# The first chunk's projection is woven with the state tiles of the other three chunks

## The chip, the cores and the metric

One core of one Trainium2 chip runs the whole program. The metric is the device time of one execution in microseconds (us). Engines are named as in the profile: PE (TensorE), ACT (ScalarE), DVE (VectorE), POOL (GpSimd), SP (SyncE, which here only issues DMAs). About 0.5% of this kernel's time is what a measurement of it can tell from no change.

## The reference, cut to what matters

```python
x = x + attn(cond(x, itok_B_0_15, W), attention weights in 4 bits with scales)   # x is 32 x 64 x 1024
x = x + ffn(cond2(x, ...), ...)
# cond: out[b,d,t] = sum over c of x[b,c,t] * W[condition[b]][c,d]: "states", one 64 x 64 block per batch row
# attn: q, k, v = states @ dequantized weights; rope; causal softmax over 64 positions; output projection
```

The change lies wholly in the beginning: the states, and the first projection of attention. Everything from the first attention step on, and the whole of the second line, is as it was.

## The kernel before, in words

The 2048 tokens are four chunks of 512. The states of a chunk are eight tiles of 128 x 512, numbered n = 8c + k over all chunks (n = 0 to 31). A state tile goes through three engines: PE makes it in a PSUM bank with four fp32 matmuls (L1420; a record counts two passes for each); ACT writes its fp16 part (L1166, count `cond_hi`), DVE the fp16 remainder (L636, count `cond_split`), and then the bank is free. Seven banks take turns.

Each chunk needs a scale before ACT may convert its first tile: DVE takes the largest magnitude of the chunk's x (`chunk_max`, L544 on y), POOL reduces it over partitions (L499), DVE makes a power of two of it in five tiny steps (`chunk_scale`, L615 and L548 to L551). The 4-bit weights of the first value head are dequantized by DVE, ACT, DVE in turn (L535, L1143, L540). The weights of the first query and key units come as ten integer pieces that ACT converts (`first_int`, L1151).

The first projection multiplies the first chunk's states by five units of weights ("k" and four query heads; units 0 to 4), eight products each. A product is two fp16 matmuls (L1435, L1437) into the unit's bank; after each of the first seven, ACT rescales the bank in place (L1182), and the next product waits for it. Two units run side by side in 24 rounds: unit 0 in rounds 0 to 7, 1 in 4 to 11, 2 in 8 to 15, 3 in 12 to 19, 4 in 16 to 23. Units 0 and 3 share a bank, so do 1 and 4. In rounds 20 to 23 PE adds a block of the values, 24 matmuls (L1447). DVE rotates each finished unit (rope: L704, L714, L716, L761, L752, L765; six instructions); for unit 3 ACT takes one of the six. Between them DVE takes the largest magnitudes of a weight matrix of the second half, eight loads through two buffers (`absmax` of `wb_stage`, L544 on work); SP issues load k when the reduction k - 2 is done (L419). After all eight, L1008 closes this stage on DVE, and DVE goes on to the first attention step.

All of these are streams written out by hand, one per engine, in order; semaphores tie them. POOL, after the four reductions of L499, fills y with zeros, a chunk at a time (L507), each once that chunk's states are made. SP issues the loads in order too: x by chunks (L344), the blocks of W for each chunk (L324, a DMA for every half block, after a register load), the pieces of the value head (L355, L356) and the integer pieces (L386).

What matters most of the order before is in PE's stream: all 32 state tiles, then a wait for the last remainder, then the rounds:

```python
pe.wait_ge(S["cond_split"], NC * KT)
for r in range(ROUNDS):
```

Of the kernel before, what the change touches and what calls it, by code (L numbers as in the profile page):

```python
# [12 lines left out]
P = 128  # L13
KT = H // P
# [39 lines left out]
def build(nc, x, cond_rep, ids_rep, seq_rep, len_rep, cond_w, s_q, s_q_cols, s_o_cols, s_k, s_v, s_o, q_q, q_k, q_v, q_o,  # L54
# [8 lines left out]
    with ctx:  # L63
# [175 lines left out]
        def col(n, k=1):  # L239
            return sc[:, n:n + k]  # L240
# [57 lines left out]
            return ((lambda part: w2h[:, part, :], w2_t, col(SC2 + 2)),  # L298
                    (lambda part: wrh[:, part, :, :].rearrange("p k e -> p (k e)"), small[:, 256:320], col(SC2 + 1)))

        cond_banks = [pj[0], pj[1], ex, cx[0], cx[1], sa, sbk]

        cond_banks = [pj[0], pj[1], ex, cx[0], cx[1], sa, sbk]

        def cond_bank(n):
            return cond_banks[n % len(cond_banks)]

        def ctx_src(e):
            return cx[e][:, :].rearrange("p (m s) -> p m s", s=SEQ)
# [19 lines left out]
        def _(sp):  # L329
# [18 lines left out]
            def load_piece(g, i):  # L348

                rows = 4 * P * i  # L350
                shape = "p (k n) -> p k n"
                src = q_v[rows:rows + 4 * P, ds(g * HD, HD)].rearrange("(k p) n -> p k n", p=P)
                scale = s_v[4 * i:4 * i + 4, ds(g * HD, HD)].partition_broadcast(P)
                need(sp, S["dq_scaled"], g * PIECES + (i - 1))
                sp.dma_start(stage[:, i, 0, :].bitcast(i32).rearrange(shape, k=4), src).then_inc(staged[i], 16)  # L355
                sp.dma_start(stage[:, i, 1, :].rearrange(shape, k=4), scale).then_inc(staged[i], 16)  # L356
# [25 lines left out]
            def load_first_ints(b):  # L382

                for p in range(*INT_BATCHES[b]):
                    dst = int_first[:, p, :] if p < 8 else int_stage[p % 2]
                    sp.dma_start(dst.rearrange("p (k n) -> p k n", k=4), int_source(0, p)).then_inc(int_first_in[b], 16)  # L386

            def load_scales(g):
                src = s_q_cols[ds(g * HD, HD), :]
                if not isinstance(g, int):  # L390
                    sp.wait_ge(S["sc_step"], g * 4)
                sp.dma_start(sc_raw[:, :], src).then_inc(S["sc_raw_in"], 16)
# [4 lines left out]
            for c in range(NC):  # L397
                with sp.Fori(CT * c, CT * (c + 1)) as i:
                    load_cond(sp, i, 0, c)
                    if c >= ACT_CHUNKS:  # L400
                        load_cond(sp, i, 1, c)
                if c + 1 < NC:
                    load_x(c + 1)
                if c == 0:
                    load_scales(0)
                    load_piece(0, 0)
                    load_piece(0, 1)
                if c < len(INT_BATCHES):
                    load_first_ints(c)
            for dst, src in ((cos_t, rope_cos), (sin_t, rope_sin), (mask_t, neg_mask), (id16, ident16)):  # L410
                sp.dma_start(dst[:, :], src).then_inc(S["consts_in"], 16)
            load_out_scales(0)
# [109 lines left out]
        def _(dve):  # L522
# [8 lines left out]
            def dequant_scale(g, i):  # L531
                slot = i % 2
                dve.wait_ge(staged[slot], 32 * g + 32)
                need(dve, S["w_ready"], PIECES * g + (i - 1))
                dve.scalar_tensor_tensor(out=w32[:, slot, :], in0=stage[:, slot, 0, :].bitcast(i32), scalar=-8.0,  # L535
                                         in1=stage[:, slot, 1, :], op0=ALU.add, op1=ALU.mult).then_inc(S["dq_scaled"], 1)
# [24 lines left out]
            def scales_inverted(g):  # L561

                dve.wait_ge(S["sc_raw_in"], 16 * g + 16)
                dve.tensor_single_scalar(sc_inv[:, :].bitcast(i32), sc_raw[:, :].bitcast(i32), 0x7FFFFFFF,
                                         ALU.bitwise_and).then_inc(S["sc_step"], 1)
                dve.wait_ge(S["sc_step"], 4 * g + 1)
                for n, lo, hi in ((1, 0, KT), (0, KT, NU * KT)):
                    dve.tensor_scalar(sc_safe[:, lo:hi], sc_inv[:, lo:hi], col(FLOOR + n), col(FLOOR2 + n), ALU.is_lt,
                                      ALU.mult).then_inc(S["sc_step"], 1)
                dve.wait_ge(S["sc_step"], 4 * g + 3)  # L570
                dve.tensor_tensor(sc_safe[:, :], sc_safe[:, :], sc_raw[:, :], ALU.add).then_inc(S["sc_step"], 1)
                dve.wait_ge(S["sc_step"], 4 * g + 4)
                dve.reciprocal(sc_inv[:, :], sc_safe[:, :]).then_inc(S["sc_inv"], 1)
# [33 lines left out]
            def chunk_max(c):  # L607
                dve.wait_ge(x_in[c], 16)
                absmax(stat[:, T_X + c:T_X + c + 1], y[:, CT * c:CT * (c + 1), :].rearrange("p i n -> p (i n)")).then_inc(S["stat_x"], 1)
# [15 lines left out]
            dve.wait_ge(S["w_scales_ready"], 1)  # L625
            chunk_max(0)
            chunk_scale(0)
            for c in range(NC):

                for k in range(KT):  # L630
                    n = c * KT + k
                    if k == (KT // 4 if c == 0 else 0) and c + 1 < NC:
                        chunk_max(c + 1)
                    dve.wait_ge(S["cond_hi"], n + 1)
                    t = slice(CH * c, CH * (c + 1))
                    dve.scalar_tensor_tensor(out=hid[:, 1, k, t], in0=cond_bank(n)[:, :], scalar=col(SH + c),  # L636
                                             in1=hid[:, 0, k, t], op0=ALU.mult, op1=ALU.subtract).then_inc(S["cond_split"], 1)
                if c == 0:
                    scales_inverted(0)
                    unit_ratios(0, 0, 3)  # L640
                    unit_ratios(0, 3, NU)
                if c + 1 < NC:
                    chunk_scale(c + 1)
                if c == 0:
                    dequant_scale(0, 0)
                    dequant_scale(0, 1)
                    dequant_split(0, 0)
                    dequant_split(0, 1)
            def score_factors():

                link(dve.tensor_scalar(col(A, NC), col(ISH, NC), 1.0 / QKV_DOWN, None, ALU.mult))
# [341 lines left out]
                    ahead = (g, c + 1) if c + 1 < NC else (None if last else (g + 1, 0))  # L993
                    step((g, c), ahead, None if first and c == 0 else (g, c - 1), between, pieces)

            score_factors()
            for u in range(NU - 1):
                rope_cos((0, 0), u)
                rope_sin((0, 0), u)
                rope_add((0, 0), u)  # L1000
                if u in (0, 1, 2):
                    rope_high((0, 0), u)
                rope_split((0, 0), u)
                for k in (2 * u, 2 * u + 1):
                    dve.wait_ge(wb_in[k % 2], 16 * (k // 2 + 1))
                    absmax(wbmax[:, k:k + 1], wb_stage[k % 2]).then_inc(S["wb_read"], 1)
            dve.wait_ge(S["wb_read"], WB_STATS)
            dve.reduce_max(stat[:, T_WB:T_WB + 1], wbmax, X).then_inc(S["stat_wb"], 1)  # L1008
            dve.wait_ge(S["y_zero"], NC)
# [128 lines left out]
        def _(act):  # L1138
# [19 lines left out]
                with act.Fori(CT * c, CT * (c + 1)) as i:  # L1158
                    load_cond(act, i, 1, c)

            for c in range(NC):
                act.wait_ge(S["h_scale_ready"], c + 1)
                for k in range(KT):
                    n = c * KT + k
                    act.wait_ge(S["cond_done"], n + 1)
                    act.activation(hid[:, 0, k, CH * c:CH * (c + 1)], cond_bank(n)[:, :], ACT.Copy,  # L1166
                                   scale=col(SH + c)).then_inc(S["cond_hi"], 1)
                act.wait_ge(S["w_scales_ready"], 1)
                if c == 0:
                    for i in range(PIECES):  # L1170
                        dequant_hi(0, i)
                else:
                    for p in range(*INT_BATCHES[c - 1]):
                        first_int(p)

            def rescale(p4, u, j):

# [165 lines left out]
            for r in range(ROUNDS):  # L1343
                for u, j in quanta(r):
                    if j < KT - 1:
                        rescale((0, 0), u, j)
                if r in (22,):
                    rope_high((0, 0), {22: 3}[r])
            group(0, first=True)
            with act.Fori(1, NKV - 1) as g:  # L1350
                group(g)
# [57 lines left out]
        def _(pe):  # L1409
            mm = nc.tensor.matmul  # L1410

            for c in range(NC):
                pe.wait_ge(x_in[c], 16)
                pe.wait_ge(wc_in[c], 16 * CB)
                for k in range(KT):
                    n = c * KT + k
                    if n >= len(cond_banks):
                        pe.wait_ge(S["cond_split"], n - len(cond_banks) + 1)
                    for i in range(CT):
                        last = mm(cond_bank(n)[:, P * i:P * (i + 1)], y[:, CT * c + i, P * k:P * (k + 1)],  # L1420
                                  wc[:, CT * c + i, :], start=True, stop=True)
                    last.then_inc(S["cond_done"], 1)

            PARTS = ((0, 0), (0, 1), (1, 0))

# [251 lines left out]
                    step((g, c), (g, c + 1) if c + 1 < NC else (None if last else (g + 1, 0)),  # L1677
                         None if first and c == 0 else (g, c - 1), turn if last and c == NC - 1 else nothing)

            pe.wait_ge(S["consts_in"], 64)  # L1680
            pe.wait_ge(S["cond_split"], NC * KT)
            for r in range(ROUNDS):
                for u, j in quanta(r):
                    quantum((0, 0), u, j)
                if r >= ROUNDS - CT:
                    value_block((0, 0), r - (ROUNDS - CT))
            group(0, first=True)
            with pe.Fori(1, NKV - 1) as g:
                group(g)
# [160 lines left out]
```

## Time and profile before

| what | value |
|---|---|
| median of 3 runs (lowest, highest) | 1920.22 us (1913.91, 1923.56) |
| profiled execution: its time, its span | 1917.04 us, 1915.0 us |
| PE, DVE, ACT, POOL busy over the span | 90%, 83%, 73%, 3% |
| mean granted clock of PE | 0.976 |
| states: first matmul to last remainder | 13.45 to 80.0 us |
| first projection: first product to the end of its stage on DVE | 80.10 to 117.98 us |

Times in the trace are counted from the start of the span. A share of busy time is an average over the whole span; the change concerns the first 118 us of it, where the shares are others (the table of stretches below). A PE matmul's record holds its pipeline, so that two that follow each other overlap; the pitch, from one start to the next, is what PE spends.

### The profile page before, as it was taken

To read this page: it belongs to the slowest core of one execution; us is meant where nothing else is said; L and a number is where in the kernel's file an instruction comes from. 1 tells how busy PE (TensorE), PEld (TensorE's weight loads), DVE (VectorE), ACT (ScalarE), POOL (GpSimd) and SP (SyncE) were. 2 spreads that over 40 slices of the span, in tenths; PEclk is the share of its full clock that TensorE was granted. 3 is DMA by queue.
4 is the path that set the end of the run, shared out by engine and by line. 5 is a ranking of instruction groups with operands and counts; after the bars stand their busy time and mean duration, and the time that the engine had idled before them with its cause. 6 is when DMAs were issued, how large, how long until landed. Compare 5 with 4: busy or idle time off the path is not lost. (4 is left out here: it accounts for less than half of the span.)

```text
span 1915.0 us, 38654 instructions
## 1 busy us (share of the span) xinstructions
PE 1722.9 (90%) x14306; PEld 942.5 (49%) x14306; DVE 1585.7 (83%) x2670; ACT 1394.6 (73%) x2361; POOL 55.6 (3%) x50
## 2 busy tenths in 40 slices
PE   3689999998999999999989999999999777779999
PEld 3435555544454455445545544454555455554444
DVE  6598999998999899989998998989998868992222
ACT  2568888988888888888888988888988527960000
POOL 0200000000000000000000000000000001320000
PEclk8799999999999999999999999999999978999999
DMA  7321111020103010200111020103020230111111
GB/s 212 100 78 35 34 46 46 1 69 12 46 1 78 4 45 19 61 25 24 34 47 46 2 75 6 46 1 78 12 58 11 89 110 23 40 40 45 44 44 44
DMA packets 118063, 87.67 MB, mean 46 GB/s; under 512 B 13404, under 2 KB 108004, under 8 KB 117860
## 3 DMA queue, kind: packets, MB, share of 16 engines
q1 hardware_dynamic: 117220, 84.83, 15.0%
q8 instruction: 128, 2.10, 0.5%
q14 instruction: 75, 0.61, 0.1%
q10 hardware_dynamic: 640, 0.13, 0.0%
HBM read 76.55 MB, written 8.39 MB: 44 GB/s over the span
## 5 line engine op out<-in xcount | busy, mean ns | idle before, releaser
L1182 ACT ACTIVATE pj<-pj,ratio 128x512 f32<-128x512 f32 x865 | 576.4, 685 | 108.1 <-PE pj L1437 102.3
L1435 PE MATMUL pj<-hid,wts 128*128 128x512 f16 x1024 | 392.1, 383 | 67.1 <-DVE pj L804 25.0
L1437 PE MATMUL pj<-hid,wts 128*128 128x512 f16 x1024 | 390.3, 381 | 0.0
L1191 ACT ACTIVATE sbk<-sbk,wts 128x512 f32<-128x512 f32 x384 | 262.4, 683 | 41.5 <-PE sbk L1504 36.6
L1191 ACT ACTIVATE sa<-sa,wts 128x512 f32<-128x512 f32 x384 | 261.1, 680 | 24.1 <-PE sa L1504 23.9
L1435 PEld LDWEIGHTS pj<-hid,wts 128*128 128x128 f16 x1024 | 99.8, 97 | 237.2 <-ACT pj L1182 72.7
L1447 PEld LDWEIGHTS tp<-wts,hid 128*128 128x128 f16 x3072 | 181.7, 98 | 32.5 <-issue 3.5
L1447 PE MATMUL tp<-wts,hid 128*128 128x128 f16 x3072 | 192.5, 219 | 0.5
L1437 PEld LDWEIGHTS pj<-hid,wts 128*128 128x128 f16 x1024 | 100.6, 98 | 76.6 <-issue 1.1
L704 DVE SCALAR_TENSOR_TENSOR work<-pj,ratio,cos_t 128x512 f32<-128x512 f32 x128 | 95.5, 746 | 45.0 <-PE pj L1437 35.8
L1182 ACT ACTIVATE ex<-ex,ratio 128x512 f32<-128x512 f32 x193 | 128.1, 664 | 3.8 <-PE ex L1437 1.2
L795 DVE SCALAR_TENSOR_TENSOR y<-sa,wts,y 128x512 f32<-128x512 f32 x128 | 95.1, 743 | 27.2 <-PE sa L1504 27.2
L761 DVE TENSOR_TENSOR work<-work 128x512 f32<-128x512 f32 x160 | 109.6, 685 | 1.7
L1502 PE MATMUL sa<-cb,wts 128*128 128x512 f16 x256 | 97.6, 381 | 8.8 <-DVE y L795 6.5
L795 DVE SCALAR_TENSOR_TENSOR y<-sbk,wts,y 128x512 f32<-128x512 f32 x128 | 95.6, 747 | 11.9 <-PE sbk L1504 10.9
L1502 PE MATMUL sbk<-wts 128*128 128x512 f16 x256 | 98.8, 386 | 7.3 <-DVE y L795 7.3
L1502 PE MATMUL sa<-wts 128*128 128x512 f16 x256 | 98.4, 384 | 7.6 <-DVE y L795 7.5
L1502 PE MATMUL sbk<-cb,wts 128*128 128x512 f16 x256 | 97.8, 382 | 4.4 <-ACT sbk L1191 4.4
L714 DVE SCALAR_TENSOR_TENSOR work<-pj,ratio,sin_t 64x512 f32<-64x512 f32 x128 | 96.7, 755 | 4.1
L1435 PE MATMUL ex<-hid,wts 128*128 128x512 f16 x256 | 98.0, 383 | 1.0 <-ACT ex L1182 1.0
L1504 PE MATMUL sa<-wts 128*128 128x512 f16 x256 | 98.3, 384 | 0.0
L1504 PE MATMUL sbk<-wts 128*128 128x512 f16 x256 | 98.2, 383 | 0.0
(243 smaller groups left out, 3184.5 us busy)
## 6 DMA issues: line engine op xcount, KB each, us to landing
wts<-qo_d SPq DMA_DIRECT2D x64, 256.0 KB, 3.2
y<-x_d SPq DMA_DIRECT2D x7, 2048.0 KB, 7.9
wts<-qq_d SPq DMA_DIRECT2D x35, 256.0 KB, 3.1
int_even<-qq_d SPq DMA_DIRECT2D x29, 256.0 KB, 2.9
out_d<-y SPq DMA_DIRECT2D x12, 512.0 KB, 2.6
work<-qv_d SPq DMA_DIRECT2D x16, 256.0 KB, 7.5
work<-sv_d SPq DMA_DIRECT2D x16, 256.0 KB, 9.5
work<-wb_d SPq DMA_DIRECT2D x8, 512.0 KB, 4.4
```

The costliest lines, as they stand in the source:

```text
L704: dve.scalar_tensor_tensor(out=rope_sum_of(u), in0=src, scalar=ratio[:, last:last + 1], in1=tables(cos_t, CB), op0=ALU.mult, op1=ALU.mult)
L714: dve.scalar_tensor_tensor(out=b[0:half], in0=src[half:HD], scalar=ratio[half:HD, last:last + 1], in1=sin_t[half:HD, :].unsqueeze(1).broad ...
L761: dve.tensor_tensor(ra[:, u % 2, :], ra[:, u % 2, :], rb[:, :], ALU.add).then_inc(S["rope_sum"], 1)
L795: dve.scalar_tensor_tensor(out=dst, in0=out_bank[t % 2][:, :], scalar=o_last[:, at:at + 1], in1=dst, op0=ALU.mult, op1=ALU.add).then_inc(y ...
L1182: act.activation(unit_bank[u][:, :], unit_bank[u][:, :], ACT.Copy, scale=ratio[:, KT * u + j:KT * u + j + 1]).then_inc(u_scaled[u], 1)
L1191: act.activation(out_bank[t % 2][:, :], out_bank[t % 2][:, :], ACT.Copy, scale=o_ratio[:, REP * t + h:REP * t + h + 1]).then_inc(o_scaled[ ...
L1435: mm(bank[:, :], w_int[:, u, j, :], hid[:, 0, j, CH * c:CH * (c + 1)], start=j == 0, stop=False, skip_group_check=True)
L1437: mm(bank[:, :], w_int[:, u, j, :], hid[:, 1, j, CH * c:CH * (c + 1)], start=False, stop=True, skip_group_check=True).then_inc(u_done[u], 1)
L1447: last = mm(shared[:, P * i:P * (i + 1)], hid[:, lw, k, CH * c + P * i:CH * c + P * (i + 1)], w_v[:, lh, k, :], start=(k == 0 and (lw, lh) ...
L1502: mm(out_bank[lane][:, :], w_out[:, h, P * t:P * (t + 1)], cbs[c % 2][:, 0, h, :], start=h == 0, stop=False, skip_group_check=True)
L1504: mm(out_bank[lane][:, :], w_out[:, h, P * t:P * (t + 1)], cbs[c % 2][:, 1, h, :], start=False, stop=True, skip_group_check=True).then_inc ...
```

## The change

Only the first chunk's eight tiles come ahead of the first projection. The other 24 (n = 8 to 31) stand in its 24 rounds, one a round, behind the round's products, on PE, ACT and DVE alike. They take four banks in turn (cx1, sa, sbk, cx0) which the projection doesn't use. With them go the integer pieces, the dequantization of the value weights (round 10), the scales of chunk 2 (round 5) and chunk 3 (round 13), the rotation of units 0, 1, 2 (rounds 8, 12, 16) and four of the eight reductions of the weight matrix (rounds 20 to 23). On SP the four loads of the value pieces move from behind x of chunk 1 to behind the integer pieces of the second batch.

```diff
-        cond_banks = [pj[0], pj[1], ex, cx[0], cx[1], sa, sbk]
+        cond_first = [pj[0], pj[1], ex, cx[0], cx[1], sa, sbk, cx[0]]
+        cond_later = [cx[1], sa, sbk, cx[0]]
 
         def cond_bank(n):
-            return cond_banks[n % len(cond_banks)]
+            return cond_first[n] if n < KT else cond_later[n % 4]
...
                 if c == 0:
                     load_scales(0)
+                if c < len(INT_BATCHES):
+                    load_first_ints(c)
+                if c == 1:
                     load_piece(0, 0)
                     load_piece(0, 1)
-                if c < len(INT_BATCHES):
-                    load_first_ints(c)
...
+            for n in range(KT):
+                cond_lo(n)
+            scales_inverted(0)
+            unit_ratios(0, 0, 3)
+            unit_ratios(0, 3, NU)
+            chunk_max(1)
+            chunk_scale(1)
...
+            for r in range(ROUNDS):
+                cond_lo(KT + r)
+                if r == 5:
+                    chunk_max(2)
+                    chunk_scale(2)
+                if r == 10:
+                    dequant_scale(0, 0)
+                    dequant_scale(0, 1)
+                    dequant_split(0, 0)
+                    dequant_split(0, 1)
+                if r == 13:
+                    chunk_max(3)
+                    chunk_scale(3)
+                if r in (8, 12, 16):
+                    first_rope(r // 4 - 2)
+                if r >= 20:
+                    wb_max(r - 20)
+            score_factors()
+            first_rope(3)
+            for k in range(4, WB_STATS):
+                wb_max(k)
...
+            for n in range(KT):
+                cond_high(n)
+            for p in range(2):
+                first_int(p)
...
+                cond_high(KT + r)
+                if r % 4 >= 2 and r < 16:
+                    first_int(2 + 2 * (r // 4) + r % 4 - 2)
+                if r == 10:
+                    act.wait_ge(S["w_scales_ready"], 1)
+                    dequant_hi(0, 0)
+                    dequant_hi(0, 1)
...
+                if n >= KT - 1:
+                    pe.wait_ge(S["cond_split"], n - 3)
...
+            for n in range(KT):
+                cond(n)
+            pe.wait_ge(S["cond_split"], KT)
             for r in range(ROUNDS):
                 for u, j in quanta(r):
                     quantum((0, 0), u, j)
+                cond(KT + r)
                 if r >= ROUNDS - CT:
                     value_block((0, 0), r - (ROUNDS - CT))
+            pe.wait_ge(S["consts_in"], 64)
+            pe.wait_ge(S["cond_split"], NC * KT)
             group(0, first=True)
```

PE's stream before, where the first chunk's eighth tile is made (hid is the states, cb the blocks of W, y is x, wts the weights):

```order
L1420 MATMUL pj0<-cb,y 128x128 x4
L1420 MATMUL pj1<-cb,y 128x128 x4
L1420 MATMUL ex<-cb,y 128x128 x4
L1420 MATMUL cx0<-cb,y 128x128 x4
L1420 MATMUL cx1<-cb,y 128x128 x4
```

The same place now, in lines of the changed kernel (L1442 makes a state tile, L1457 and L1459 are a product):

```order
L1442 MATMUL cx0<-cb,y 128x128 x4
L1457 MATMUL pj0<-hid,wts 128x512
L1459 MATMUL pj0<-hid,wts 128x512
L1442 MATMUL cx1<-cb,y 128x128 x4
L1457 MATMUL pj0<-hid,wts 128x512
L1459 MATMUL pj0<-hid,wts 128x512
L1442 MATMUL sa<-cb,y 128x128 x4
```

Before, 24 more tiles came there ahead of the first product; now a product stands ahead of each of them.

DVE's stream before at the end of the stage: the last rotation, its two reductions, L1008, and the first instruction of the attention step:

```order
L704 SCALAR_TENSOR_TENSOR work<-pj0,ratio,cos_t 128x512
L714 SCALAR_TENSOR_TENSOR work<-pj0,ratio,sin_t 64x512
L716 SCALAR_TENSOR_TENSOR work<-pj0,ratio,sin_t 64x512
L761 TENSOR_TENSOR work<-work 128x512
L765 TENSOR_TENSOR qb<-work,qb 128x8x64
L544 TENSOR_REDUCE stat<-work 128x1 x2
L1008 TENSOR_REDUCE stat<-stat 128x1
L704 SCALAR_TENSOR_TENSOR work<-pj1,ratio,cos_t 128x512
```

DVE's stream now, from the last two remainders on (L633 a remainder, L646 the first of the five score factors, L699 to L760 the rotation, L1025 what L1008 was):

```order
L633 SCALAR_TENSOR_TENSOR hid<-sbk,sc,hid 128x512
L544 TENSOR_REDUCE stat<-work 128x1
L633 SCALAR_TENSOR_TENSOR hid<-cx0,sc,hid 128x512
L544 TENSOR_REDUCE stat<-work 128x1
L646 TENSOR_SCALAR sc<-sc 128x4
...
L699 SCALAR_TENSOR_TENSOR work<-pj0,ratio,cos_t 128x512
...
L760 TENSOR_TENSOR qb<-work,qb 128x8x64
L544 TENSOR_REDUCE stat<-work 128x1 x4
L1025 TENSOR_REDUCE stat<-stat 128x1
```

Two reductions stood behind each rotation; now the first four stand between the last remainders and the other four behind the last rotation.

## Rows read from the trace of the kernel before

**Rows 1.** Busy time by stretch: PE, PEld, DVE, ACT, POOL, then PEclk, DMA share, GB/s.
```profile
60.00:80.00 20.00, 10.99 (x72) 10.53 (x72) 14.54 (x23) 9.21 (x15) 12.14 (x5) 0.74 0.31 93
...
100.00:120.00 20.00, 16.95 (x158) 8.73 (x158) 18.93 (x25) 12.47 (x21) 0.35 (x1) 1.00 0.42 136
```
**Rows 2.** Timeline of the states: start, length, instruction, count, and the wait before it.
```profile
12.18 4.42 DVE L544 TENSOR_REDUCE stat<-y 128x1 f32<-128x4096 f32 x1 [0.96 <-DMA y<-x_d]
...
17.86 0.15 DVE L551 TENSOR_SCALAR sc<-bits 128x1 f32<-128x1 f32 x1
...
21.16 4.41 DVE L544 TENSOR_REDUCE stat<-y 128x1 f32<-128x4096 f32 x1
...
26.14 1.40 DVE L636 SCALAR_TENSOR_TENSOR hid<-cx,sc,hid 128x512 f16<-128x512 f32 x2
...
29.43 0.17 DVE L564 TENSOR_SCALAR sc_inv<-sc_raw 128x40 int32<-128x40 int32 x1
...
31.63 0.15 DVE L615 SCALAR_TENSOR_TENSOR sc<-top 128x1 f32<-128x1 f32 x1
...
35.29 2.05 PE L1420 MATMUL pj<-cb,y 128*128 128x128 f32 x8 [12.21 <-issue]
...
38.75 1.95 PE L1420 MATMUL cx<-cb,y 128*128 128x128 f32 x16
...
51.46 2.05 PE L1420 MATMUL ex<-cb,y 128*128 128x128 f32 x8 [2.81 <-issue]
...
53.60 0.69 ACT L1166 ACTIVATE hid<-ex,sc 128x512 f16<-128x512 f32 x1 [2.16 <-PE ex L1420]
...
69.58 3.55 PE L1420 MATMUL cx<-cb,y 128*128 128x128 f32 x16 [4.21 <-issue]
```
**Rows 3.** Timeline of SP's loads of the value pieces, and of their dequantization on DVE.
```profile
12.85 0.69 SPq L355 DMA_DIRECT2D work<-qv_d  x1
...
17.82 2.97 SPq L386 DMA_DIRECT2D wts<-qk_d  x2
...
32.57 1.29 DVE L535 SCALAR_TENSOR_TENSOR work<-work 128x512 f32<-128x512 int32 x2
...
34.11 1.42 DVE L540 SCALAR_TENSOR_TENSOR wts<-work,sc,wts 128x512 f16<-128x512 f32 x2 [0.25 <-ACT wts L1143]
```
**Rows 4.** Timeline of DVE in the first projection: rotations, weight reductions, the end.
```profile
98.43 0.74 DVE L704 SCALAR_TENSOR_TENSOR work<-pj,ratio,cos_t 128x512 f32<-128x512 f32 x1
...
102.53 2.34 DVE L544 TENSOR_REDUCE stat<-work 128x1 f32<-128x1024 f32 x2
104.79 0.74 DVE L704 SCALAR_TENSOR_TENSOR work<-ex,ratio,cos_t 128x512 f32<-128x512 f32 x1
...
117.82 0.16 DVE L1008 TENSOR_REDUCE stat<-stat 128x1 f32<-128x8 f32 x1
```
**Rows 5.** Timeline of PE in the first projection: a product, value blocks.
```profile
84.54 0.61 PE L1435 MATMUL pj<-hid,wts 128*128 128x512 f16 x1 [0.75 <-ACT pj L1182]
...
109.27 1.50 PE L1447 MATMUL tp<-wts,hid 128*128 128x128 f16 x24
110.61 0.38 PE L1435 MATMUL pj<-hid,wts 128*128 128x512 f16 x1
...
111.04 1.50 PE L1447 MATMUL tp<-wts,hid 128*128 128x128 f16 x24
```
**Rows 6.** Loads of the weight matrix: count, KB each, median us to landing.
```profile
work<-wb_d SPq DMA_DIRECT2D x8, 512.0 KB, 4.4
```
**Rows 7.** Timeline of POOL's zero fills, and of DVE's score factors.
```profile
62.90 10.48 POOL L507 MEMSET y<- 128x4096 f32 x3
...
78.55 3.51 POOL L507 MEMSET y<- 128x4096 f32 x1 [5.18 <-PE cx L1420]
...
79.92 2.17 DVE L651 TENSOR_SCALAR sc<-sc 128x4 f32<-128x4 f32 x1
...
82.12 0.23 DVE L652 TENSOR_SCALAR sc<-sc 128x4 f32<-128x4 f32 x1
```

More of the change, by code:

```diff
@@ L299, in small_parts @@
                     (lambda part: wrh[:, part, :, :].rearrange("p k e -> p (k e)"), small[:, 256:320], col(SC2 + 1)))
-        cond_banks = [pj[0], pj[1], ex, cx[0], cx[1], sa, sbk]
-        cond_banks = [pj[0], pj[1], ex, cx[0], cx[1], sa, sbk]
+        cond_first = [pj[0], pj[1], ex, cx[0], cx[1], sa, sbk, cx[0]]
+        cond_later = [cx[1], sa, sbk, cx[0]]
         def cond_bank(n):
-            return cond_banks[n % len(cond_banks)]
+            return cond_first[n] if n < KT else cond_later[n % 4]
         def ctx_src(e):
@@ L627, in _, with cond_lo @@
             chunk_scale(0)
[L628 to L648, printed above, removed]
+            def cond_lo(n):
+                c, k = n // KT, n % KT
+                t = slice(CH * c, CH * (c + 1))
+                dve.wait_ge(S["cond_hi"], n + 1)
+                dve.scalar_tensor_tensor(out=hid[:, 1, k, t], in0=cond_bank(n)[:, :], scalar=col(SH + c),
+                                         in1=hid[:, 0, k, t], op0=ALU.mult, op1=ALU.subtract).then_inc(S["cond_split"], 1)
+            for n in range(KT):
[5 more added lines that the diff above has]
+            chunk_scale(1)
             def score_factors():
@@ L994, in group, with first_rope @@
                     step((g, c), ahead, None if first and c == 0 else (g, c - 1), between, pieces)
-            score_factors()
-            for u in range(NU - 1):
+            def first_rope(u):
                 rope_cos((0, 0), u)
@@ L1003, in _, with wb_max @@
                 rope_split((0, 0), u)
-                for k in (2 * u, 2 * u + 1):
-                    dve.wait_ge(wb_in[k % 2], 16 * (k // 2 + 1))
-                    absmax(wbmax[:, k:k + 1], wb_stage[k % 2]).then_inc(S["wb_read"], 1)
+            def wb_max(k):
+                dve.wait_ge(wb_in[k % 2], 16 * (k // 2 + 1))
+                absmax(wbmax[:, k:k + 1], wb_stage[k % 2]).then_inc(S["wb_read"], 1)
+            for r in range(ROUNDS):
[19 more added lines that the diff above has]
+                wb_max(k)
             dve.wait_ge(S["wb_read"], WB_STATS)
@@ L1159, in _, with cond_high @@
                     load_cond(act, i, 1, c)
-            for c in range(NC):
+            def cond_high(n):
+                c, k = n // KT, n % KT
                 act.wait_ge(S["h_scale_ready"], c + 1)
[L1163 to L1174, printed above, removed]
+                act.wait_ge(S["cond_done"], n + 1)
+                act.activation(hid[:, 0, k, CH * c:CH * (c + 1)], cond_bank(n)[:, :], ACT.Copy,
+                               scale=col(SH + c)).then_inc(S["cond_hi"], 1)
+            for n in range(KT):
+                cond_high(n)
+            for p in range(2):
+                first_int(p)
             def rescale(p4, u, j):
@@ L1346, in _ @@
                         rescale((0, 0), u, j)
-                if r in (22,):
-                    rope_high((0, 0), {22: 3}[r])
+                cond_high(KT + r)
[5 more added lines that the diff above has]
+                    dequant_hi(0, 1)
+            rope_high((0, 0), 3)
             group(0, first=True)
@@ L1410, in _, with cond @@
             mm = nc.tensor.matmul
[L1412 to L1422, printed above, removed]
+            def cond(n):
+                c, k = n // KT, n % KT
+                if k == 0:
+                    pe.wait_ge(x_in[c], 16)
+                    pe.wait_ge(wc_in[c], 16 * CB)
+                if n >= KT - 1:
+                    pe.wait_ge(S["cond_split"], n - 3)
+                for i in range(CT):
+                    last = mm(cond_bank(n)[:, P * i:P * (i + 1)], y[:, CT * c + i, P * k:P * (k + 1)],
+                              wc[:, CT * c + i, :], start=True, stop=True)
+                last.then_inc(S["cond_done"], 1)
             PARTS = ((0, 0), (0, 1), (1, 0))
@@ L1678, in group @@
                          None if first and c == 0 else (g, c - 1), turn if last and c == NC - 1 else nothing)
-            pe.wait_ge(S["consts_in"], 64)
-            pe.wait_ge(S["cond_split"], NC * KT)
+            for n in range(KT):
+                cond(n)
+            pe.wait_ge(S["cond_split"], KT)
             for r in range(ROUNDS):
```

## Prediction

> **What bounds the kernel now.** I read the stretches of busy time first, then the timelines of the beginning. The two stretches shown [rows 1] differ: from 60 to 80 us PE is busy 11.0 of 20 us, DVE 14.5, ACT 9.2, and PE's granted clock is 0.74 on average, so part of it at the lower level (1.2 of 2.4 GHz); from 100 to 120 us DVE is busy 18.9, PE 17.0. So the states wait, and the first projection is full. The timeline of the states says for what. PE starts chunk 1 at 35.29 after 12.21 us of idleness, chunk 2 at 51.46, the last eight tiles at 69.58, each time after idle time [rows 2]: it waits for W's blocks or for banks. A chunk's scale costs DVE 5.83 us (12.18 to 17.86 + 0.15) [rows 2]. In the projection DVE goes without a pause from a rotation (98.43) to two reductions (102.53) to the next rotation (104.79), and L1008 ends the stage at 117.82 + 0.16 = 117.98 [rows 4]. That is the number to move: the attention step behind it is unchanged and waits for DVE there.
>
> **The change part by part.** No arithmetic goes away; the sum is the new end of L1025, by a walk along the stream that is late at each point. Prices: a remainder 0.70 (1.40 for two), a conversion or rescaling on ACT 0.69 [rows 2], a rotation 4.10 (98.43 to 102.53), a reduction 1.13 (102.53 to 104.79, two) [rows 4], dequantization 2.96 (32.57 to 34.11 + 1.42) [rows 3]. On PE a state tile takes 0.98 at the upper clock level (1.95 for two), 1.73 at the lower (35.29 to 38.75, two) [rows 2], a product 0.43 (110.61 to 111.04), a block of values 1.34 (109.27 to 110.61) [rows 5]. At the lower level I double the last two: 84.54 shows a single matmul at 0.61 against 0.38 [rows 5].
>
> Opening. Chunk 1's maximum (4.41) stood inside the first eight remainders, which ended at 29.43; now they end at 25.0. Inverses and ratios take 2.2 (29.43 to 31.63) [rows 2]: 27.2. Maximum and scale of chunk 1: 27.2 + 5.83 = 33.0. W's blocks for chunk 1 don't bind: four loads of value pieces (12.85 to 17.82, 4.97 us) [rows 3] leave SP's queue ahead of them, so they come near 35.3 - 5.0 = 30.3. The moved loads go behind chunk 1's blocks and still ahead of chunk 2's, so those come near 51.4 as before.
>
> Rounds 0 to 7. ACT's first conversion of chunk 1 ends at 33.7. A round of one product is ACT-bound at the upper clock (two activations and the hand-over back, about 2.0 us) and PE-bound at the lower (0.86 + 1.73 = 2.6); of two products 2.1 (three activations) to 3.4 (1.72 + 1.73). Rounds 1 to 3 and 4, 5 take 10.2 to 14.6; I take 11, since a round in which PE is busy throughout is what put the clock up before (1.73 a tile, then 0.98 [rows 2]). Chunk 2's maximum then starts at about 45.5 and its scale is there at 51.3, when its blocks land too. PE will have been idle, so I let the first tile run as before, with ACT's conversion at 53.60 to 54.29 [rows 2].
>
> Rounds 8 to 16, DVE's. From 54.3: a remainder and unit 0's rotation, 59.1; two remainders, 60.5; dequantization, 63.5. Here a new wait appears: ACT, in order, stands in round 10 at the conversion of the dequantized half until DVE has made it (60.5 + 0.65), is free at 62.6 after two of 0.69, and then has four activations for round 11 (a piece among them) and three for round 12, 4.83 us: 67.4. Behind it wait all rescalings, and so PE. DVE is idle some 3 us there. Then on DVE: remainder and rotation of unit 1, 72.2; remainder, maximum and scale of chunk 3, 78.7 (blocks for chunk 3 came at 69.58 before [rows 2] and don't bind); three remainders, 80.8; rotation of unit 2, 84.9; three more, 87.0.
>
> Rounds 17 to 23. ACT, held by chunk 3's scale, goes on at 78.7: conversion, two rounds of three activations, one of two: 84.9. From there PE is the slow one: 0.43 + 0.98 + 1.34 = 2.75 a round, tile 31 at 85 + 3 x 2.75 + 1.4 = 94.6; converted 95.5, remainder 96.2. DVE's reductions lie beside: the first ends at 88.8, the second 91.6; a load takes 4.4 from its issue [rows 6], and is issued when the reduction two earlier ends: third 88.8 + 4.4 + 1.1 = 94.3, fourth 97.3.
>
> End. Score factors, five at about 0.24 [rows 7], 1.2: 98.5. But POOL fills the last chunk of y from tile 31 on for 3.51 [rows 7], until 98.2, and L651 before, the first of the five, took 2.17 and ended with the fill (78.55 + 3.51 = 82.06, 79.92 + 2.17 = 82.09), where its like at 82.12 took 0.23 [rows 7]: 0.9 more, 99.4. Rotation 103.5; two reductions 104.6, 105.8; the seventh waits for its load, 104.6 + 4.4, ends 110.1; the eighth 111.3; L1025 111.5. Against 117.98 that is 6.5 less. PE has then been idle some 13 us and restarts at the lower level: the first 24 small matmuls and products cost about 0.5 to 1 more. Net gain 6.
>
> The cast in unit 2's rotation now falls at 83.8, into the fills of the first three chunks (10.48 for three [rows 7], from about 77.5). No row shows a cast beside a fill. From both sides: nothing, as most of DVE's work beside fills before; or until the fills end, 88.0, 4.2 us. I take 0.8, the end of the running fill, most of which the PE-bound rounds hide. The Trainium skill (SBUF — State Buffer, "SBUF: two separate sides") says that VectorE and GpSimd share a port pair which one holds for a whole instruction while the other blocks. L651's row agrees. By the rule, a cast that reads one SBUF tensor fast waits at least for the running fill: the end would be up to 4.2 us later, the gain 2 to 6; if only L651's kind of instruction is held, it stays 6.
>
> The sum: 1917.04 - 6 = 1911. The profiled execution is 3.2 below the median of 1920.22; off the median the same gain gives 1914.
>
> **The rivals.**
> 1. More is gained. My two holes (ACT in round 10, PE in rounds 20 to 23) are read off a chain, not a trace. If DVE runs through from 53.6, its work is 16 remainders 11.2, four rotations 16.4, dequantization 2.96, chunk 3 5.83, eight reductions 9.0, factors and L1025 1.4: 46.8, 100.4, and 3.3 for the last load's wait: 103.7. Gain 14; with half the holes 11: 1906. For it: DVE is the fuller engine from 100 to 120 us. Against: three streams in order, each held by the other two.
> 2. Nothing is gained: the wait only moves. Rounds 0 to 5 at the lower clock (scale of chunk 2 3.5 us later) and the fills' full 4.2 leave -1 to 3: 1916. For it: the clock in the states was low; against: half of that delay is hidden by the blocks at 51.4.
> 3. Slower: PE stays at the lower level through the rounds. Place: rounds 0 to 23; price: four rounds of 2.6, sixteen of 3.45, four of 0.86 + 1.73 + 2.68 = 5.3, sum 87, from 33.0 to 120; tile 31 at 117, and the tail behind it as above (16.9 us) ends L1025 at 134: 16 later, 1933. It decides once a round takes over about 2.9 us on average (117.98 - 16.9 + 2.7 - 33.0 = 71 over 24). For it: 84.54 shows the lower level within the old rounds. Against: there PE was busy a third of the time; with a tile in each round at the lower level PE would never pause.
> 4. The change doesn't do what it says: if chunk 1's blocks came late after all (SP's stream held by its loads), rounds 1 to 7 would start at 35 to 38, and the scale of chunk 2 at 53 to 56: gain 1 to 4, inside case 2.
>
> **How the numbers follow.** My forecast (gain 3 to 9.6) has 0.52, rival 1 (over 9.6) 0.28, rivals 2 and 4 0.13, rival 3 and other losses 0.07. The bound of 0.5%, which is what a measurement tells from no change, is 9.6 us: faster 0.28; same 0.52 + 0.13 = 0.65; slower 0.07. Range: the lower end a gain of 16 (rival 1 and a little from the clock), 1901; the upper takes in no gain and the median's 3 us offset, 1921; rival 3 stays outside.
>
> **What would show it.** Right: a first product at about 25 us; ACT's first conversion of chunk 1 near 33; chunk 2's scale and blocks both near 51; ACT held in round 10 by L535's successor; DVE the late one from 54 to 85; the seventh weight reduction waiting on its load; L1025 ending at 109 to 113. Wrong: chunk 2's tiles well off 51, no wait on ACT in round 10, a granted clock of 0.5 through 55 to 95 us, a cast of several us at 84, or L1025 beyond 118.

## The result, and the profile after

The changed kernel is slower: 1948.46 us (1947.21 to 1949.72, 4 runs) against 1921.89 (1913.91 to 1923.94, 4 runs) of the kernel before, a ratio of 1.0143 [1.0125, 1.0161]. The forecast was 1911. The changed kernel's profiled execution took 1948.12 us, with a span of 1946.1. Four executions in the experiments below, one of the kernel before and three of experiment 4, took 2059 to 7910 us and are left out of every median and ratio.

The first place to look is the busy time by stretch, of the kernel after (PE, PEld, DVE, ACT, POOL, then PEclk, DMA share, GB/s). The stretches 60:80 and 100:120 answer to [rows 1].

```profile
40.00:60.00 20.00, 0.26 (x2) 0.00 (x0) 0.00 (x0) 1.49 (x3) 0.00 (x0) 0.62 0.58 164
60.00:80.00 20.00, 10.74 (x61) 7.85 (x62) 8.69 (x8) 7.77 (x13) 0.35 (x1) 0.70 0.14 37
...
100.00:120.00 20.00, 13.68 (x122) 10.56 (x121) 19.22 (x22) 11.04 (x19) 10.69 (x4) 1.00 0.00 1
```

From 40 to 60 us the core computes next to nothing: DVE has no instruction at all, PE 0.26 us, ACT 1.49. That isn't a slower engine but one wait that holds all. The waits of the stretch 20:150 name it (engine, line, what it waited for, us in total, times, longest):

```profile
DVE hid L633 <- DMA id<-id_d: 35.0, 1, 35.0
ACT hid L1183 <- PE cx L1442: 34.0, 5, 29.8
PE cx L1442 <- DVE hid L633: 29.7, 2, 28.8
```

DVE's remainder L633 waits 35.0 us for the load of `id`, the identity table. But L633 reads a bank, a scale and a state: it has no use for `id`. PE waits for DVE, and ACT for PE: the four banks of the state tiles hold tiles that ACT has converted, and only a remainder frees a bank. The timeline of the kernel after (start, length, engine, instruction, and the idle time before it with what ended it):

```profile
25.39 0.39 PE L1457 MATMUL pj<-hid,wts 128*128 128x512 f16 x1 [1.63 <-DVE hid L633]
...
33.10 0.15 DVE L551 TENSOR_SCALAR sc<-bits 128x1 f32<-128x1 f32 x1
...
33.29 0.69 ACT L1183 ACTIVATE hid<-cx,sc 128x512 f16<-128x512 f32 x1 [5.38 <-DVE sc L551]
...
66.35 0.43 SPq L411 DMA_DIRECT2D id<-id_d  x1
...
68.30 0.75 DVE L633 SCALAR_TENSOR_TENSOR hid<-cx,sc,hid 128x512 f16<-128x512 f32 x1 [35.04 <-DMA id<-id_d]
...
69.10 1.22 PE L1442 MATMUL cx<-cb,y 128*128 128x128 f32 x4 [28.84 <-DVE hid L633]
...
80.63 0.15 DVE L551 TENSOR_SCALAR sc<-bits 128x1 f32<-128x1 f32 x1
...
105.50 10.47 POOL L507 MEMSET y<- 128x4096 f32 x3
...
111.62 4.63 DVE L747 CAST qb<-work 128x512 f16<-128x512 f32 x1
...
141.70 0.16 DVE L1025 TENSOR_REDUCE stat<-stat 128x1 f32<-128x8 f32 x1
```

Up to 33.29 all runs as forecast: the first product at 25.39, the scale of chunk 1 at 33.25, where the walk had 33.0. Then the remainder of tile 8 stands until 68.30, chunk 2's scale comes at 80.78 instead of 51.3, and the stage ends at 141.86 instead of 117.98 [rows 4]: 23.9 of the 26.6 us between the medians.

The wait that holds L633 stands on neither side of the diff. DVE's stream is written by functions and by bare statements between them, and one of these is the line `dve.wait_ge(S["consts_in"], 64)` (L839 before, L834 after): from here on the four tables (cos, sin, mask, `id`) are there. It stands ahead of the function `step`, and nobody moved it. Before, the remainders and scales of all chunks stood ahead of it, and what came behind it was L651, the first score factor. The change placed the rounds, and with them the remainders from tile 8 on, behind it. PE has a wait of its own for the same tables, and the diff does move that one, from ahead of the rounds (L1680 before) to behind them (L1711 after). The first instruction that carries the wait, before and now, with the semaphores that it waits for:

```
L651 TENSOR_SCALAR sc<-sc 128x4 [waits consts_in]
L633 SCALAR_TENSOR_TENSOR hid<-cx,sc,hid 128x512 [waits cond_hi,consts_in,h_scale_ready]
```

In the kernel before, SP issued the last table at 69.57 and DVE came to the wait at 79.9, with no idle time ahead of it (L651 in [rows 7] has no bracket). The timeline of the kernel before:

```profile
69.57 0.43 SPq L411 DMA_DIRECT2D id<-id_d  x1
...
79.25 0.75 DVE L636 SCALAR_TENSOR_TENSOR hid<-cx,sc,hid 128x512 f16<-128x512 f32 x1
```

SP loads the tables behind all blocks of W, chunk 3's too, so their date hardly moved (69.57 to 66.35); the instruction that asks for them moved from 79.9 to 33.3.

### The profile page after: what moved, and what is told of

Same layout as the page of the kernel before. It is cut to its first block and busy times, and to the rows that moved or that the text cites. A ratio compares the mean times of both kernels' runs of the same rounds, so it can differ in the third digit from the quotient of the medians.

```text
span 1946.1 us, 38679 instructions
## 1 busy us (share of the span) xinstructions
PE 1717.7 (88%) x14306; PEld 943.5 (48%) x14306; DVE 1588.4 (82%) x2670; ACT 1392.3 (72%) x2361; POOL 55.6 (3%) x50
## 5 line engine op out<-in xcount | busy, mean ns | idle before, releaser
L1457 PE MATMUL pj<-hid,wts 128*128 128x512 f16 x1024 | 393.1, 384 | 77.2 <-DVE pj L799 25.0
L1459 PE MATMUL pj<-hid,wts 128*128 128x512 f16 x1024 | 391.1, 382 | 0.0
L1457 PEld LDWEIGHTS pj<-hid,wts 128*128 128x128 f16 x1024 | 100.1, 98 | 238.7 <-ACT pj L1197 66.7
L1459 PEld LDWEIGHTS pj<-hid,wts 128*128 128x128 f16 x1024 | 100.9, 99 | 78.0 <-issue 1.9
L699 DVE SCALAR_TENSOR_TENSOR work<-pj,ratio,cos_t 128x512 f32<-128x512 f32 x128 | 95.7, 748 | 36.0 <-PE pj L1459 26.8
L1524 PE MATMUL sbk<-wts 128*128 128x512 f16 x256 | 99.0, 387 | 8.5 <-DVE y L790 8.5
L1457 PE MATMUL ex<-hid,wts 128*128 128x512 f16 x256 | 99.0, 387 | 6.6 <-ACT ex L1197 6.6
L1459 PE MATMUL ex<-hid,wts 128*128 128x512 f16 x256 | 98.8, 386 | 0.0
```

Source lines behind the costliest of these rows:

```text
L699: dve.scalar_tensor_tensor(out=rope_sum_of(u), in0=src, scalar=ratio[:, last:last + 1], in1=tables(cos_t, CB), op0=ALU.mult, op1=ALU.mult)
L1457: mm(bank[:, :], w_int[:, u, j, :], hid[:, 0, j, CH * c:CH * (c + 1)], start=j == 0, stop=False, skip_group_check=True)
L1459: mm(bank[:, :], w_int[:, u, j, :], hid[:, 1, j, CH * c:CH * (c + 1)], start=False, stop=True, skip_group_check=True).then_inc(u_done[u], 1)
L1524: mm(out_bank[lane][:, :], w_out[:, h, P * t:P * (t + 1)], cbs[c % 2][:, 0, h, :], start=h == 0, stop=False, skip_group_check=True)
```

## Experiments

Two theories at first: the wait is the whole loss, and the rest of the walk holds (then the tables' date, or the wait's place, sets the end of the stage); or the interleaved stage is slower by itself, through PE's clock or the fills (rival 3 of the prediction), and the wait hides a part of it. All ratios are to the kernel before in the same comparison (medians 1916.72 us for experiments 1 to 4, 1922.36 for 5 to 7 and the first run of 8, 1920.4 for the second runs of 3 and 8). The expected times count from the result's 1921.89, so in 1 to 4 they lie some 5 us high, and the ratio is the better measure.

**1. The wait alone moved to where the tables are used.** Ahead of the first rotation; the loads stay.

```diff
-            dve.wait_ge(S["consts_in"], 64)
...
+                if r == 8:
+                    dve.wait_ge(S["consts_in"], 64)
```

> The changed kernel with DVE's wait for the four constant tables moved from ahead of round 0 to the first rotation, in round 8; the loads stay where they were (landing near 68 us). Theory (the wait for the tables holds DVE from 33 to 68 us, and with it conversion banks and PE): remainders of chunk 1 run from 34 us, chunk 2's scale is there near 51, and only the first rotation stands until 68.3 instead of starting at 82.8, so the end of the stage on DVE (141.86 in the changed kernel) comes 14 to 17 us earlier, at 125 to 128; time 1931 to 1934. Rival A (the stand-still is of another cause, such as W's blocks for chunk 3 or the loading of code): DVE still stands until 68, time 1948. Rival B (the weaving itself is slow): rounds 0 to 7 take the time that the wait took, time over 1942.

Measured: 1926.12 us, ratio 1.0042 [1.0027, 1.0057]. Timeline of this kernel:

```profile
68.49 0.75 DVE L699 SCALAR_TENSOR_TENSOR work<-pj,ratio,cos_t 128x512 f32<-128x512 f32 x1 [16.10 <-DMA id<-id_d]
...
126.95 0.16 DVE L1025 TENSOR_REDUCE stat<-stat 128x1 f32<-128x8 f32 x1
```

The wait went with its line to the rotation and shrank to 16.10 us; the stage ends 14.8 us earlier than in the kernel after, inside what was expected. The time was 5 us under the expected range, by as much as the kernel before was lower here.

**2. The tables loaded one chunk earlier,** ahead of chunk 3's blocks; the wait stays.

```diff
-            for dst, src in ((cos_t, rope_cos), (sin_t, rope_sin), (mask_t, neg_mask), (id16, ident16)):
-                sp.dma_start(dst[:, :], src).then_inc(S["consts_in"], 16)
+                if c == 2:
+                    for dst, src in ((cos_t, rope_cos), (sin_t, rope_sin), (mask_t, neg_mask), (id16, ident16)):
+                        sp.dma_start(dst[:, :], src).then_inc(S["consts_in"], 16)
```

> The changed kernel with the loads of the four tables moved up in SP's stream, ahead of W's blocks for chunk 3 (SP reaches that place at 51.5 us); the wait on DVE stays where it was. Theory: the stand-still of DVE ends when the tables land, near 55 instead of 68.3, and everything behind shifts with it: end of the stage near 129, time about 1935. Rival A (another cause): no change, 1948. Rival B: somewhere between, since rounds are slow whatever the wait.

Measured: 1932.9 us, ratio 1.0076 [1.0061, 1.0091]. Timeline of this kernel:

```profile
54.32 0.43 SPq L412 DMA_DIRECT2D id<-id_d  x1
...
58.59 0.75 DVE L634 SCALAR_TENSOR_TENSOR hid<-cx,sc,hid 128x512 f16<-128x512 f32 x1 [25.34 <-DMA id<-id_d]
...
132.87 0.16 DVE L1026 TENSOR_REDUCE stat<-stat 128x1 f32<-128x8 f32 x1
```

The remainder goes when the tables are there, now at 58.59: 9.7 earlier than in the kernel after, and the stage ends 8.8 earlier, at 133.03 (expected were 55 and 129; the tables landed later than that). The date of a load that L633 does not read moves the end of the stage.

**3. The tables loaded first,** behind the scales of chunk 0. This takes the wait off, and leaves the change as the prediction had understood it. Run again later (the second expectation).

```diff
                 if c == 0:
                     load_scales(0)
+                    for dst, src in ((cos_t, rope_cos), (sin_t, rope_sin), (mask_t, neg_mask), (id16, ident16)):
+                        sp.dma_start(dst[:, :], src).then_inc(S["consts_in"], 16)
...
-            for dst, src in ((cos_t, rope_cos), (sin_t, rope_sin), (mask_t, neg_mask), (id16, ident16)):
-                sp.dma_start(dst[:, :], src).then_inc(S["consts_in"], 16)
```

> The changed kernel with the loads of the four tables right behind the scales, ahead of the first integer pieces (SP is there at 12.8 us; four issues of 0.47). Theory: DVE never waits for the tables, and the walk of the prediction applies, with the cast of unit 2 held for up to 4.2 us: end of the stage 111 to 116, time 1913 to 1920, that is 28 to 35 below the changed kernel and -9 to 0 against before. Rival A: DVE still stands until 68, 1948. Rival B: the rounds are slower than the walk, time 1925 or more.

> The run with the tables first once more, on one chip with the run that has all moves, since the two were timed on different chips (ratios to the kernel before 0.9971 and 0.9941). Theory: 0.996 to 0.998 again.

Measured: 1911.64 us, ratio 0.9971 [0.9959, 0.9983], and again 1913.6, ratio 0.9961 [0.9947, 0.9976]. Timeline of the first, the points of the walk:

```profile
34.05 0.75 DVE L633 SCALAR_TENSOR_TENSOR hid<-cx,sc,hid 128x512 f16<-128x512 f32 x1 [0.87 <-ACT hid L1183]
...
50.93 0.15 DVE L551 TENSOR_SCALAR sc<-bits 128x1 f32<-128x1 f32 x1
51.12 0.69 ACT L1183 ACTIVATE hid<-cx,sc 128x512 f16<-128x512 f32 x1 [1.38 <-DVE sc L551]
...
58.52 1.28 DVE L535 SCALAR_TENSOR_TENSOR work<-work 128x512 f32<-128x512 int32 x2
59.30 1.34 ACT L1160 ACTIVATE wts<-work,sc 128x512 f16<-128x512 f32 x2 [3.50 <-DVE work L535]
...
65.65 0.75 DVE L633 SCALAR_TENSOR_TENSOR hid<-cx,sc,hid 128x512 f16<-128x512 f32 x1 [3.08 <-ACT hid L1183]
...
75.81 10.48 POOL L507 MEMSET y<- 128x4096 f32 x3
76.73 0.15 DVE L551 TENSOR_SCALAR sc<-bits 128x1 f32<-128x1 f32 x1
...
81.94 4.62 DVE L747 CAST qb<-work 128x512 f16<-128x512 f32 x1
...
95.70 0.74 DVE L633 SCALAR_TENSOR_TENSOR hid<-cx,sc,hid 128x512 f16<-128x512 f32 x1
...
98.27 0.16 DVE L646 TENSOR_SCALAR sc<-sc 128x4 f32<-128x4 f32 x1
...
99.46 0.75 DVE L699 SCALAR_TENSOR_TENSOR work<-pj,ratio,cos_t 128x512 f32<-128x512 f32 x1
...
108.54 1.22 DVE L544 TENSOR_REDUCE stat<-work 128x1 f32<-128x1024 f32 x1 [2.42 <-DMA work<-wb_d]
...
111.67 0.16 DVE L1025 TENSOR_REDUCE stat<-stat 128x1 f32<-128x8 f32 x1
...
114.53 0.61 PE L1457 MATMUL pj<-hid,wts 128*128 128x512 f16 x1
```

Its busy time by stretch (columns as above):

```profile
40.00:60.00 20.00, 14.80 (x96) 10.30 (x94) 15.90 (x22) 15.12 (x27) 0.35 (x1) 1.00 0.63 172
60.00:80.00 20.00, 15.67 (x77) 10.61 (x78) 15.71 (x22) 14.51 (x25) 4.41 (x3) 0.76 0.27 84
80.00:100.00 20.00, 15.72 (x157) 13.58 (x155) 17.94 (x22) 7.32 (x11) 9.79 (x3) 0.84 0.30 86
```

The stretch that was empty in the kernel after is busy (DVE 15.90 of 20 us), and the stage ends at 111.83, in the second run at 111.67; the walk had 111.5. Without the wait the interleaved stage is not slower than the old one, which ended at 117.98.

**4. Control: the kernel before with the tables loaded first** (the edit of 3 on it).

> The kernel before with the loads of the four tables at that early place. It is the control: there DVE came to its wait at 79.9, when the tables had landed for 8 us. Theory: no gain, 0 to +2 us (W's blocks come up to 1.9 us later), 1919 to 1924. If early tables helped here too, the gain of the run before would not be the wait's.

Measured: 1916.74 us, ratio 1.0006 [0.9993, 1.0019]; timeline of this kernel:

```profile
118.42 0.16 DVE L1008 TENSOR_REDUCE stat<-stat 128x1 f32<-128x8 f32 x1
```

The earlier loads are worth nothing in the kernel before, since there nobody waited for them. So the gain of 3 is the interleaving's.

**5. The kernel before with the wait put early.** Only DVE's wait is moved, to where the inverses begin.

```diff
+                    dve.wait_ge(S["consts_in"], 64)
...
-            dve.wait_ge(S["consts_in"], 64)
```

> The kernel before, unwoven, with nothing changed but the place of DVE's wait for the tables: ahead of the inverses behind the first chunk's remainders (29 us) instead of behind all remainders (80 us). Theory: the wait alone costs what the change lost. DVE stands from 29 until the tables land (71.5), then has some 30 us of its state work left, so the projection starts near 102 instead of 80: time 1936 to 1945. Rival (only the woven order suffers): under 1930.

Measured: 1945.39 us, ratio 1.0128 [1.0100, 1.0155]. Timeline of this kernel:

```profile
72.21 0.18 DVE L564 TENSOR_SCALAR sc_inv<-sc_raw 128x40 int32<-128x40 int32 x1 [42.77 <-DMA id<-id_d]
...
104.72 0.74 DVE L636 SCALAR_TENSOR_TENSOR hid<-cx,sc,hid 128x512 f16<-128x512 f32 x1
...
144.16 0.16 DVE L1007 TENSOR_REDUCE stat<-stat 128x1 f32<-128x8 f32 x1
```

One line in the other order of work costs nearly as much as the whole change did: 23.0 us (1945.39 - 1922.36) against 26.6. The loss needs no interleaving.

**6. The fills of y one by one,** each behind the next chunk's reduction on POOL, on top of 3, to price the cast of 4.62 us.

```diff
-            for c in range(NC):
-                over_partitions("stat_x", c + 1, T_X + c, T_X + c + 1, "top_x")
-
-            for c in range(NC):
+            def fill(c):
...
+            for c in range(NC):
+                over_partitions("stat_x", c + 1, T_X + c, T_X + c + 1, "top_x")
+                if c:
+                    fill(c - 1)
+            fill(NC - 1)
```

> The run with the tables first, and in it POOL's fills of y set between its four reductions (the fill of a chunk behind the reduction of the next) instead of behind all four. There the cast of unit 2 took 4.62 us, from 81.94 to the end of three fills, where a free one takes 0.43. Theory: no fill is then beside a cast, the cast is 0.43, DVE is 4.2 earlier at 87 us, of which the PE-bound rounds 20 to 23 hide a part: end of the stage 108 to 110 instead of 111.85, time 1.5 to 4 us below the run with the tables first. Rival (the cast is long for another reason, or all of it is hidden): cast still above 1 us, or no change in time.

Measured: 1912.45 us, ratio 0.9953 [0.9937, 0.9968]. Timeline of this kernel:

```profile
74.31 3.58 POOL L504 MEMSET y<- 128x4096 f32 x1
...
80.44 0.43 DVE L750 CAST qb<-work 128x512 f16<-128x512 f32 x1
...
108.55 0.16 DVE L1028 TENSOR_REDUCE stat<-stat 128x1 f32<-128x8 f32 x1
```

With no fill running, the cast takes 0.43 again, and the stage ends at 108.71, 3.1 earlier than in 3. The time can't be told from 3's: the intervals of the ratios overlap.

**7. Six reductions and the last rotation earlier,** on top of 3, to take DVE's waits for the loads out of the tail.

```diff
+                if r in (16, 17, 18, 20):
+                    wb_max({16: 0, 17: 1, 18: 2, 20: 3}[r])
...
-                if r >= 20:
-                    wb_max(r - 20)
+                if r == 21:
+                    first_rope(3)
+                if r in (21, 23):
+                    wb_max({21: 4, 23: 5}[r])
```

> The run with the tables first, and in it the weight reductions 0 to 3 in rounds 16, 17, 18 and 20 instead of 20 to 23, unit 3's rotation with reduction 4 in round 21, reduction 5 in round 23, and only the score factors and reductions 6 and 7 behind the rounds. In the run with the tables first, DVE needs 15.4 us from the last remainder (96.4) to the end (111.85), 4.9 of them in waits for loads. Theory: that tail shrinks to about 6 us, end of the stage 103 to 106, time 6 to 9 below the run with the tables first, 1903 to 1906. Rival (the moved work delays the remainders, and PE behind them, by as much): within 2 us of the run with the tables first.

Measured: 1911.85 us, ratio 0.9945 [0.9925, 0.9965]; the stage ended at 110.21, not at 103 to 106. Timeline of this kernel:

```profile
95.48 0.74 DVE L699 SCALAR_TENSOR_TENSOR work<-pj,ratio,cos_t 128x512 f32<-128x512 f32 x1
...
103.30 0.75 DVE L633 SCALAR_TENSOR_TENSOR hid<-cx,sc,hid 128x512 f16<-128x512 f32 x1 [1.65 <-ACT hid L1186]
...
110.05 0.16 DVE L1028 TENSOR_REDUCE stat<-stat 128x1 f32<-128x8 f32 x1
```

That is the expectation's rival: the moved work stands ahead of remainders which release banks, the last one went from 95.70 to 103.30, and what the tail saved was mostly lost there. By its time it can't be told from 3 either.

**8. Both, with chunk 3's scale two rounds earlier and the dequantization spread** over rounds 10 to 13 (DVE's first half in 10, ACT's in 12, DVE's second in 13). Run again beside the second run of 3. On top of 6 and 7, in DVE's rounds (ACT's conversion of its half goes from round 10 to 12):

```diff
                 if r == 10:
                     dequant_scale(0, 0)
                     dequant_scale(0, 1)
-                    dequant_split(0, 0)
-                    dequant_split(0, 1)
-                if r == 13:
+                if r == 11:
                     chunk_max(3)
                     chunk_scale(3)
+                if r == 13:
+                    dequant_split(0, 0)
+                    dequant_split(0, 1)
```

> Both of these, and besides the scale of chunk 3 in round 11 instead of 13, and the dequantization taken apart: DVE's first half stays in round 10, ACT converts in round 12, DVE ends it in round 13, so that ACT doesn't wait in round 10 (3.5 us in the run with the tables first). Theory: all terms of the walk count where their stream is late: end of the stage 100 to 104, time 1900 to 1904, about 1% below the kernel before. Rival (PE's own rounds at a mixed clock set the pace): no better than the run with the early reductions alone.

> The run with all moves once more beside it. By the profiles its stage ends on DVE at 106.6 instead of 111.85 us: theory 4 to 6 us below the run with the tables first (0.2 to 0.3%). Rival (the difference was the chips'): within 1.5 us of it.

Measured: 1908.97 us, ratio 0.9941 [0.9918, 0.9963], and again 1905.35, ratio 0.9920 [0.9905, 0.9935], 8.25 below the kernel of 3 in the same comparison, where 4 to 6 were expected. Timeline of the second:

```profile
67.19 3.51 POOL L504 MEMSET y<- 128x4096 f32 x1 [2.62 <-PE cx L1450]
...
69.25 1.73 DVE L750 CAST qb<-work 128x512 f16<-128x512 f32 x1
...
104.07 0.16 DVE L1032 TENSOR_REDUCE stat<-stat 128x1 f32<-128x8 f32 x1
```

The stage ends at 104.23, 13.8 earlier than before. It is the fastest version, and beats both kernels. The first run missed what was expected of it: its stage ended at 106.59 instead of 100 to 104, and its time was 1908.97 instead of 1900 to 1904. Why the two profiles of one kernel end the stage 2.4 us apart is not shown.

## Why the prediction was wrong

**The step that failed** is "Rounds 0 to 7". It begins with ACT's first conversion of chunk 1 at 33.7 and lets the remainders follow. The conversion came (33.29 + 0.69), but the remainder behind it stood until 68.30. The walk followed the waits of the moved instructions on each other; it did not list the waits that were left standing between the old and the new place. The sign was there: the diff has a line `pe.wait_ge(S["consts_in"], 64)` behind PE's rounds, and none for DVE. Of SP's queue it asked where the moved loads go, not what in DVE's stream waits for the loads that were not moved. Experiment 1 shows that the wait is the line's, 2 that its price follows the tables' date, 5 that it costs nearly as much without the rest of the change.

**Why 35.0 us of waiting cost 30.0.** Without the wait (experiment 3) the first remainder of chunk 1 stood at 34.05 and the stage ended at 111.83; with it, 68.30 and 141.86. The 34.25 at the start are 30.0 at the end. The difference comes back in rounds 0 to 5: chunk 2's scale follows the first remainder by 12.5 us (68.30 to 80.78) against 17.0 (34.05 to 51.08) without the wait, where the remainders wait for ACT one by one; with it, ACT had converted four tiles by 39.85, and their remainders follow each other from 68.30 without a pause. And 30.0 less the interleaving's 6.2 (117.98 to 111.83) are the 23.9 lost. The other 2.7 of the medians' difference I can't place. From the stage's end to the end of the span the profiled runs took 1797.0 (before), 1804.2 (after), 1797.4 (experiment 3), 1802.2 (experiment 6), 1798.7 (experiment 5), and over all twelve runs 1795.4 to 1804.2; this does not follow the edits, and I leave it open.

**What held,** by experiment 3, against the walk (forecast, measured): chunk 2's scale 51.3, 51.08. Dequantization's start 60.5, 58.52. ACT held in round 10 by L535: said, 3.50 us. DVE idle there: 3, 3.08. Chunk 3's scale 78.7, 76.88. Last remainder's end 96.2, 96.44. Rotation 3's start 99.4, 99.46. The seventh reduction waits for its load: said, 2.42 us. L1025's end 111.5, 111.83. PE's restart at the lower clock level, 0.5 to 1: after 8.00 us of idleness (13 were said) its granted clock is 0.50 from 112 to 116 us, its products take 0.61 to 0.63 from 114.53 instead of 0.38, and the next rotation starts 12.07 behind the first of the attention step against 11.04 before: 1.0. The net gain was put at 6; the two runs give 5.1 and 6.8 (1916.72 - 1911.64, 1920.4 - 1913.6).

**The cast beside the fills** had bounds of nothing and 4.2 us; I took 0.8. It was the upper bound: 4.62 against 0.43 without a fill, so 4.19. My reason, the end of the running fill, was wrong where three fills stand back to back: the cast began in the second and ended 0.27 us behind the third (75.81 + 10.48 = 86.29). Experiment 6, without it, ended the stage 3.1 earlier, but was 1.5 ahead before the cast already (80.44 against 81.94). So 1.6 to 3.1 of the 4.2 may have been paid; that rests on one profile of experiment 6, and where the rest went is not shown.

**Luck in the 111.5.** It was met partly by errors that cancel. The cast's 4.2 were not in the sum. Against them, the walk let chunk 2's first tile "run as before", converted at 53.60 to 54.29, since PE would have been idle; ACT converted it at 51.12 to 51.81, with PE's granted clock at 1.00 from 40 to 60 us, and so dequantization and chunk 3's scale came 2.0 and 1.8 sooner than the walk had them. And the score factors were not held by the last fill (0.16 at 98.27, where 0.9 more was put down).

**The rivals.** The sign was rival 3's, at 0.07, but not its mechanism (PE at the lower level through the rounds): in experiment 3 PE's granted clock was 1.00 from 40 to 60 us, 0.76 and 0.84 in the next two stretches. Rival 1 (a gain of 11 to 14) was not in this change, though experiment 8 reaches 11.4 and 13.8 at the stage's end in its two runs by closing its holes. Rival 4 comes nearest in form, a load that holds the rounds, but it looked at W's blocks alone.

## What to carry to other kernels

When work moves forward in an engine's stream, list every wait that lies between its old place and its new one, bare ones and those outside the diff included, and ask of each when its load lands: a wait that costs nothing at 80 us can cost 35 at 33. The sign in a trace is an instruction that waits for a tile it does not read. When the diff moves one engine's wait for a semaphore, look for the other engines' waits for the same one. And a load that stands late in its queue only because nobody needs it earlier has to be looked at again whenever its reader, or the wait for it, moves.

## What was not expected of the hardware

A DVE cast of a 128x512 tile to f16 that began beside POOL's zero fills lasted until all fills that stood back to back were done: 4.62 us in experiment 3, begun in the second of three fills, 4.63 in the kernel after (111.62 + 4.63 against 105.50 + 10.47, again 0.28 behind), 1.73 beside the end of a single one (experiment 8: 67.19 + 3.51 = 70.70, cast to 70.98), 0.43 with none. The scalar-tensor-tensor operations between 76.9 and 81.9 in experiment 3, beside the same fills, kept their 0.74 to 0.76, and the TENSOR_SCALAR of 128x1 at 76.73 its 0.15, while that of 128x4 was held in [rows 7]. The Trainium skill (SBUF — State Buffer, "SBUF: two separate sides") says that one of the two engines holds a shared port pair for a whole instruction. The trace agrees that the cast is shut out, and adds that the change from one fill to the next did not let it in: the three fills of experiment 3 start at 75.81, 79.26 and 82.70 and last 3.58 us each, so the third starts 0.14 before the second's end at 82.84.
